# A four-layer language-model tower on one core: the last MoE stage's units, gate and results run on in the head slots, and the tokens are cut in five parts

## The reference

```python
h = take(L0_tok_weight, x)                              # 16384 tokens x 128
h = h + linear_attention(layernorm(h))                  # 8 heads of 16, relu(q), relu(k), clipped denominator
h = h + expert_choice_ffn(layernorm(h))                 # 32 experts, each takes its best 512 tokens
h = h + causal_attention(layernorm(h), Wq, Wk, Wv, Wo)  # 64 sequences of 256, 8 heads of 128
logits = layernorm(h) @ gate_w + gate_b                 # last stage: 8 experts
vals, idx = top_k(logits, 2); w = softmax(vals)
out = h + sum over the 2 picked e of w_e * (relu(x @ w1[e] + b1[e]) @ w2[e] + b2[e])
```

## Time and profile before

| | us |
|---|---|
| median of 3 runs | 2666.74 |
| the profiled execution, its own time | 2664.6 |
| its span, first to last instruction | 2662.9 |
| causal attention with 3 parts of units, first head product to last head sum | 908.4 to 2496.5 |
| gate, scatters and table of the last part | 2496.5 to 2525.8 |
| its 56 units, to the landing of the last output | 2525.8 to 2636.3 |
| six results and the last stores | 2636.3 to 2662.9 |

### The profile page before, as it was taken

One profiled execution on the slowest core, in us unless ns is written; L12 is line 12 of the kernel. 1 busy time (PEld: TensorE's weight loads), 2 busy tenths in 40 slices (PEclk: granted clock), 3 DMA queues, 4 the chain that ended last, 5 costly groups with the idle time before them and its releaser, 6 DMA issues.

```text
span 2662.9 us, 58077 instructions
## 1 busy us (share of the span) xinstructions
PE 2256.9 (85%) x16551; PEld 2003.8 (75%) x16551; DVE 1941.9 (73%) x8859; ACT 1681.3 (63%) x5240; POOL 1178.9 (44%) x1217
## 2 busy tenths in 40 slices
PE   4888878576667599999999999999999999999473
PEld 4777755455555488888888899999989899889463
DVE  4888856644444388888888988788798888888522
ACT  4776745222222377777777788888878788778253
POOL 7555300588888302222222234444436554454343
PEclk9999989777777799999999999999999999999787
DMA  2332310244444520000000155555537754773387
GB/s 79 95 84 80 88 39 1 50 73 78 75 72 74 102 54 26 26 27 29 25 25 25 32 135 151 155 150 152 151 96 223 221 157 112 213 205 105 110 259 216
DMA packets 282605, 271.30 MB, mean 102 GB/s; under 512 B 32795, under 2 KB 232057, under 8 KB 282288
## 3 DMA queue, kind: packets, MB, share of 16 engines
q1 hardware_dynamic: 231600, 195.90, 27.1%
q0 software_dynamic: 46080, 61.16, 10.2%
q10 hardware_dynamic: 4608, 10.52, 1.3%
HBM read 182.69 MB, written 86.84 MB: 101 GB/s over the span
## 4 chain that ended last, share of the span: by engine, by line
PE 48%; DVE 25%; POOL 12%; issue 8%; DMA 3%; SPq 2%; ACT 1%; DVEq 0%; POOLq 0%; ACTq 0%
POOL hbuf L816 7%; PE bank L2148 6%; PE bank L2061 6%; PE bank L2134 5%; PE bank L2069 5%; PE bank L2101 4%; PE bank L2109 3%; POOL xe L808 3%; PE bank L2060 3%; PE bank L2081 3%; PE bank L2083 3%; PE bank L2082 3%; DVE pr_place L1550 2%; DVE nmax L1532 2%; DVE pr_place L1543 2%
## 5 line engine op out<-in xcount | busy, mean ns | idle before, releaser
L856 POOL DMA_INDIRECT spread_rows<-kb,pos x256 | 249.2, 973 | 455.1 <-ACT pr_place L1069 318.1
L870 POOL DMA_INDIRECT zbuf<-pc,kb x232 | 232.4, 1002 | 265.3 <-DVE pc L1712 214.7
L1067 ACT ACTIVATE pr_place<-bank,nmax 128x128 f32<-128x128 f32 x512 | 188.5, 368 | 218.1 <-DVE nmax L1532 215.6
L2061 PE MATMUL bank<-xT,gT 128*128 128x256 f32 x1024 | 306.3, 381 | 0.0
L2069 PE MATMUL bank<-ident,pr_place 128*128 128x128 f32 x1536 | 254.6, 275 | 52.8 <-DVE pr_place L1550 52.4
L2069 PEld LDWEIGHTS bank<-ident,pr_place 128*128 128x128 f32 x1536 | 189.3, 141 | 139.7 <-DVE pr_place L1543 72.0
L1550 DVE COPY pr_place<-bank 128x384 f32<-128x384 f32 x512 | 281.4, 550 | 1.5 <-PE bank L2069 1.4
L2148 PE MATMUL bank<-wvo_part,x_part 128*128 128x512 f32 x768 | 268.3, 457 | 0.0
L1077 ACT ACTIVATE bank<-causal 128x384 f32<-128x384 f32 x512 | 253.4, 495 | 19.7 <-PE bank L2186 3.6
L1531 DVE TENSOR_REDUCE nmax<-bank 128x1 f32<-128x128 f32 x512 | 143.5, 280 | 158.6 <-PE bank L2061 156.8
L2134 PE MATMUL bank<-x_part,wqk_part 128*128 128x256 f32 x1536 | 245.5, 296 | 1.7 <-DVE x_part L1657 1.2
(11 more groups left out here) (322 smaller groups left out, 6276.8 us busy)
## 6 DMA issues: line engine op xcount, KB each, us to landing
pa<-bundle SPq DMA_DIRECT2D x186, 321.0 KB
wu_more<-bundle SPq DMA_DIRECT2D x62, 321.0 KB
junk<-zbuf SPq DMA_DIRECT2D x32, 512.0 KB
kb<-spread_rows SPq DMA_DIRECT2D x232, 65.0 KB
xrow<-xr SPq DMA_DIRECT2D x32, 320.0 KB, 2.5
hbuf<-h SPq DMA_DIRECT2D x32, 256.0 KB, 3.0
hx<-hbuf SPq DMA_DIRECT2D x64, 128.0 KB, 2.8
h3buf<-h SPq DMA_DIRECT2D x64, 128.0 KB
```

The lines of the kernel that those rows point to most:

```text
L2061: pe.matmul(s2[:, P:3 * P], g[:, P:2 * P], xT3[:, p], start=False, stop=True, skip_group_check=True)\
```

## The change

`PORTS` has five parts in place of four: 14, 8, 5, 3 and 2 groups, with 120, 72, 48, 32 and 24 units, 296 in all in place of 288. The list of slots goes on from 512 to 591 (`NI` pairs of 16). `place_steps` gives every step a slot: part 0 from 256, part 1 from 384, part 2 from 464 to 513, part 3 from 514 to 548, part 4 from 549 to 575. The tails written by hand are gone; each engine runs the slot loop to its end, and what belongs to heads is left out after slot 511 or its lag. So the gate of group 31 is in slots 517 to 527, its scatters one a slot in 528 to 535, the last table in 528 to 534 and the last padding in slot 536.

`LOADS` names the slot of each load: four before the unit's own, and for units from 256 on five to seven before it. The rows and weights of units from `RING` = 248 on lie in the buffers of the tail before. Results of groups 0 to 21 stay with POOL in slots below 512. Those of 22 to 26 are loaded by SP in slots 520, 524, 528, 532 and 536, those of 27 to 29 in 555, 559 and 563, and each is added by DVE two slots later. Only groups 30 and 31 come behind the loop. The core of the diff:

```diff
-PORTS = ((0, 13), (13, 21), (21, 26), (26, 32))
+PORTS = ((0, 14), (14, 22), (22, 27), (27, 30), (30, 32))
+NKA = 3
...
+RING = END0 + WR
...
+    steps, at, ends, slot = [], {}, [], 0
     for k, (g0, g1) in enumerate(PORTS):
-        lags = LAGS[k == NK - 1]
+        lags = LAGS[k >= NKA]
+        slot = max(slot, (g1 + 2) * 2 * H1)
         for r in range(NUNS[k] + lags[2]):
...
+            at[slot + r] = len(steps)
+            steps.append([UNIT0[k] + r - d if 0 <= r - d < NUNS[k] else None for d in lags])
+        slot += NUNS[k] + lags[2]
+        ends.append(slot)
...
+        for t, u in SLOT_OF.items():
+            early = u - 4 if t < RING + WR else max(u - 4 - min(3, (t - RING - WR + 2) // 2), (PORTS[portion_of(t)][1] + 1) * 2 * H1 + H1 + 1)
+            LOADS.setdefault(early, []).append(t)
...
+        for k, (g0, g1) in enumerate(PORTS[:-1]):
             for g in range(g0, g1):
+                RESULT_AT[STEP_END[k] + 6 + 4 * (g - g0)] = g
...
             def load_end(t):
+                if q == 0:
+                    sp.wait_ge(head_mm, U)
+                if q >= ER:
                     sp.wait_ge(z_out[(t - ER) % YR], given(t - ER + 1, (t - ER) % YR))
...
+                if q % 2 == 0:
+                    if q < WR:
+                        sp.wait_ge(yu_ready, t - WR + 1)
...
-            for u in range(NB * H1):
+            for u in range(NI * 2 * H1):
...
                 for k in range(NK):
-                    if (i, p, h) == (PORTS[k][1] + 1, 1, 4):
+                    if (i, p, h) == (PORTS[k][1] + 1, 1, 4 if k < NK - 1 else 0):
                         pad_regions(k)
...
+                for t in LOADS.get(u, ()):
+                    (load_unit if t < RING else load_end)(t)
                 if u in RESULT_AT:
                     turn_result(RESULT_AT[u])
-            store_h(NB - 1)
-            late = len(RESULT_AT)
-            turn_result(late)
-            pad_regions(NK - 1)
-            sp.wait_ge(yu_ready, END0)
-            sp.wait_ge(head_mm, NB * H1)
-            for t in range(UNIT0[NK - 1], UNIT0[NK]):
-                load_end(t)
...
+                if i == NG + 1 and p == 0:
+                    scatter(NG - 1, h // TG, h % TG)
                 if u - 2 in STEP_AT and STEPS[STEP_AT[u - 2]][2] is not None:
                     give_unit(STEPS[STEP_AT[u - 2]][2])
...
-                if u - 2 in RESULT_AT:
+                if u - 2 in RESULT_AT and u < U:
                     add_rows(RESULT_AT[u - 2])
...
                         if u - 1 in STEP_AT:
                             unit_out(STEP_AT[u - 1])
                         for k in range(NK):
                             if i == PORTS[k][1] + 1 and p == 0 and h < TABLE_PARTS:
                                 table(k, h)
+                        if u - 2 in RESULT_AT and u >= U:
+                            results(RESULT_AT[u - 2])
```

More of the change, by code:

```diff
@@ L53, in place_steps @@
 def place_steps():
-    steps, at = [], {}
+    steps, at, ends, slot = [], {}, [], 0
     for k, (g0, g1) in enumerate(PORTS):
-        lags = LAGS[k == NK - 1]
+        lags = LAGS[k >= NKA]
+        slot = max(slot, (g1 + 2) * 2 * H1)
         for r in range(NUNS[k] + lags[2]):
[L59 to L64, removed]
+            at[slot + r] = len(steps)
+            steps.append([UNIT0[k] + r - d if 0 <= r - d < NUNS[k] else None for d in lags])
+        slot += NUNS[k] + lags[2]
+        ends.append(slot)
+    return steps, at, ends
 def first(i):
@@ L448, in end_there @@
             q = j % ER
-            return 32 * (j // ER + 1 + (len(range(q, END0, WR)) if q < WR else 0))
+            return 32 * (j // ER + 1 + (len(range(q, RING, WR)) if q < WR else 0))
         xy_mm = sem("xy_mm")
@@ L495, in lm_tower @@
         RESULT_AT = {}
[L496 to L497 removed]
+        for k, (g0, g1) in enumerate(PORTS[:-1]):
             for g in range(g0, g1):
[L499 to L500 removed]
+                RESULT_AT[STEP_END[k] + 6 + 4 * (g - g0)] = g
+        assert list(RESULT_AT.values()) == list(range(PORTS[-1][0]))
         def rounds(eng, one):
@@ L1110, in unit_step, with load_weights, heads @@
                     ins.then_inc(hTu_ready, 1)
-            def heads(i, last):
+            def load_weights(t):
+                q = t - RING
+                k = portion_of(t)
+                j = t - UNIT0[k]
+                act.wait_ge(yu_ready, t - (WR if q < WR else ER) + 1)
+                e = act.value_load(unit_x[j:j + 1, k:k + 1], min_val=0, max_val=E1 - 1)
+                act.dma_start(wu_at(t), bundle[bass.ds(e, 1)].rearrange("a p c -> (a p) c")).then_inc(end_in[q % ER], 16)
+            def heads(i):
                 for p in range(2):
@@ L1127, in heads @@
                                 .then_inc(vo_ready, 1)
-                        if h == 5 and not (last and p == 1):
+                        if h == 5 and n + 1 < NB:
                             turned(n + 1, 1 - p)
@@ L1131, in heads @@
                             exps(u - S_LAG, (h - S_LAG) % H1)
-                        if (p, h) == (1, 5) and there(i - 1):
+                        if (p, h) == (1, 5) and gated(i - 1):
                             gaps(i - 1)
[L1134 to L1161, removed]
+            for i in range(NI):
+                heads(i)
         @block.vector
@@ L1714, in unit_out, with results, slots @@
                     .then_inc(yu_ready, 1)
-            def slots(i, last):
+            def results(c):
+                p = c % 2
+                dve.wait_ge(z_in[p], 32 * (c // 2 + 1))
+                if c >= 2:
+                    dve.wait_ge(out_done[p], 16 * (c // 2))
+                dve.tensor_tensor(res[:, p], zx[:, p, :, 0:C], zx[:, p, :, C:2 * C], ALU.add).then_inc(res_step, 1)
+                dve.wait_ge(res_step, c + 1)
+                dve.tensor_tensor(res[:, p], res[:, p], h3x[:, p], ALU.add).then_inc(res_ready, 1)
+            def slots(i):
                 for p in range(2):
@@ L1720, in slots @@
                         u = H1 * n + h
-                        if h in (1, 2, 3) and not (last and p == 1):
+                        if h in (1, 2, 3) and n + 1 < NB:
                             root = [prep_root, 5 * (h - 1), 1, 1]
-                        elif p == 0 and h in (6, 7) and there(i - 1):
+                        elif p == 0 and h in (6, 7) and gated(i - 1):
                             root = [gate_root, 7 * (h - 6), 1, 2]
@@ L1760, in slots @@
                             finish(n - 1, 1 - p, i, p)
-                        if (p, h) in GATE_SLOTS and there(i - 1):
+                        if (p, h) in GATE_SLOTS and gated(i - 1):
                             GATE_SLOTS[p, h](i - 1)
```

192 lines of the change are left out of this document (66 added, 126 removed).

## The result

The changed kernel takes 2690.76 us (median of 4 runs, 2687.1 to 2692.67) where the kernel before took 2666.73 beside it (4 runs): a ratio of 1.0090, 95% interval 1.0073 to 1.0108. It is slower by 24.0 us. The profiled execution took 2692.07 us, its span is 2689.1, 26.2 above the 2662.9 of before. The forecast was 2681.3: 14.6 us slower.

What follows compares the result with a forecast made beforehand. Behind the heads, DVE's result requests and SP's row loads were taken to wait for each other in a loop. Head phase, results, outputs and end summed to 2677.5, +14.6 on the span: forecast 2681.3 us, range 2642 to 2700.

Steps and rivals of the forecast that it cites:

- the head phase: Up to the last head sum: 11 more unit steps at 0.90 us, 9.9 us, so the sum comes at 2506.4.
- the first result: Behind the heads: SP's store, seven load issues of 7.7 us, then 8.5 us for result 22, at 2523.4.
- The loop: Behind the heads: DVE's result request and SP's row load wait for each other, 14.5 us a turn of four slots.
- Result 23: Behind result 22: its SP slot waits for unit 246's output; 11.4 us, to 2534.8.
- Result 24: Behind result 23: one loop turn and the first scatter of group 31, 1.3 us; at 2550.6.
- Result 26: Behind result 24: unit 256's output, six POOL instructions, padding, landings and load; 34.8 us, to 2585.4.
- Result 27: Behind result 26: output to landing 4.9, 19 issues 20.9, then the result; 34.3 us, to 2619.7.
- Padding: In SP's slots before result 26: 8.35 us for the padding, and 2 us taken for its landing.
- Edits taken at nothing: Gate and table in passing slots, and result adds on DVE beside POOL's scatters (at most 4 us): no cost.
- A: Rival behind the heads: loop hidden, landings covered by loaded units, SP's issue the limit; span 2638.6, time 2642.4; chance 0.17.
- B: Rival behind the heads: loop there, but landings short as in the empty end; 2663.5, no difference; chance 0.18.
- C: Rival behind the heads: long landings, each result among loads SP has just issued; 2705.4; chance 0.08.

Runs made afterwards that it cites:

- e1_again: The kernel after, unchanged, run again beside the other experiments: 2689.88 us, ratio 1.0084.
- e9_four: Against the kernel after: slots run on with the early request, but tokens in the four parts of the kernel before, 288 units: 2668.99 us, ratio 1.0011.
- e3_behind: Against the kernel after: results 22 to 29 taken out of the slots, all ten last results behind the last unit: 2664.67 us, ratio 0.9997.
- e2_late6: Against the kernel after: DVE asks for each late result six slots behind SP's load, not two: 2662.56 us, ratio 0.9987.
- e5_late3: Against the kernel after: DVE asks for late results three slots behind SP's load, not two: 2678.16 us, ratio 1.0039.
- e8_all: Against the kernel after: requests six slots behind, last paddings one by one and awaited in slot 537, row ring of 18 places: 2663.94 us, ratio 0.9989.
- e10_wait: Against the kernel after: requests six slots behind, last paddings one by one, awaited in slot 542; third chip: ratio 0.9998.
- e13_wait: Same kernel as e10_wait, run again on the third chip: ratio 0.9980.
- e11_late4: Against the kernel after: DVE asks for late results four slots behind SP's load, not two; third chip: ratio 1.0033.
- e12_late4: Same kernel as e11_late4, run again on the third chip: ratio 1.0029.

## Why the prediction was right, point by point

The direction and the mechanism held: the time of 2690.8 lies within 2642 to 2700, 9.5 above the forecast. By spans the forecast was 14.6 and 26.2 was measured; three steps carry the 11.6: 7.4 from the head phase and 5.0 from the first result, less 0.8 on the whole way behind it. That the sum came so close is in part luck, as the first point shows. By place, 16.6 of the 26.2 lie before slot 512's transposes, and only 9.6 behind them.

- **The loop.** Predicted 14.5 for a turn; measured 13.9 to result 25, 15.3 to result 28, 13.3 to result 29 (e1_again 14.1, 15.1, 12.8). Its terms were off in ways that nearly cancel: the output's landing 2.90 and 2.96 for 3.7, the result's 7.71 and 5.54 for 6.0. Result 23: 13.0 for 11.4. Result 24: 16.2 for 15.8. Result 26, with the padding: 33.4 for 34.8. Result 27: 33.9 for 34.3. Last landing 16.1 for 16.2, the end 12.3 for 12.6. From result 22 to the end of the span it was 153.3 us, forecast 154.1.
- **The head phase** failed by 7.4: DVE's `finish` of the last head came at 2513.82, not 2506.4. Of this 4.8 were there before slot 240 (see the last section). The stretch of slots 240 to 512 grew by 11.8 against the earlier trace rows where six steps at 0.90 gave 5.4: more steps, but also more results beside steps (22 where 19 stood). The eight profiles of five parts on the first chips, whose slots are the same there, have 947.0 to 951.8, so this execution is near the upper end, and some of the miss is its own. In e9_four, which has the steps and results of before there, it was 938.7, so the growth belongs to the new parts; what each of steps and results costs was not parted. The drained slots gave 3.8 back: 5.9 us against 5.2, where I added 4.5, so the four steps that stand ahead of the last head sum were nearly free there (I had counted five; the fifth is behind it).
- **The first result** failed by 5.0: 22.0 us from `finish` to result 22's adds, forecast 17.0. I had SP stand at slot 517's store, ready. The timeline of SP in the kernel after shows it behind its own issues:

```profile
2515.34 0.34 SPq L646 DMA_DIRECT2D pa<-bundle  x1
2516.54 0.34 SPq L644 DMA_DIRECT2D kb<-spread_rows  x1
2517.63 0.34 SPq L646 DMA_DIRECT2D wu_more<-bundle  x1
2518.01 0.43 SPq L679 DMA_DIRECT2D h3buf<-h  x1
```

  In this stretch a slot has two issues, 2.25 us, while the slots themselves passed in 1.47. SP came to the store 3.8 us after I had it there; seven further issues took 8.2 for 7.7, and the result 9.15 for 8.5. So part of the price of the four drained slots stands in SP's queue, where I had put nothing.
- **Padding** cost near what the earlier trace rows said: 8.01 us of issues for 8.35, and a landing of 1.58 (I took 2). The kernel after, SP's queue and chain:

```profile
2580.74 8.01 SPq L630 DMA_DIRECT2D spread_rows<-padrow  x8
```

```profile
2588.42 1.58 DMA spread_rows<-padrow
```

- **Edits taken at nothing.** The gate and table in slots did not show on the path. The adds on DVE beside POOL's scatters did not either: the scatters behind results 27 and 28 took 0.97 us each, not the 1.35 and 1.50 of the earlier trace rows. The rule of the Trainium skill on that (SBUF — State Buffer, Who interferes with whom) did not come into play, for POOL stood waiting for DVE during the adds. In e3_behind, where one scatter did run beside them, it took 1.32 us.
- **The rivals.** A (hidden, 2642.4) did not come, and e2_late6 shows that it does not come even with the request out of the way. Its span is 19.3 above A's 2638.6: SP had issued the loads of 247 to 250 at 2522.2, not 2514.9, which is 7.3; from there to the end of the last row load it took 109.2 us, where A's sum of SP's issues has 98.3, which is 10.9 more. In this stretch the DMA engines were at 0.92, 0.96, 0.72 and 0.93, a limit that A left out; that it makes all of the 10.9 was not tried. My line that no row showed a landing under 4.6 held for results alone: an output's was 2.11. B and C priced all landings at one end; those read in the chain between results 24 and 29 were 4.6 to 7.7 for results and 2.9 to 4.2 for outputs, so neither end held. The Trainium skill (DMA: Bandwidth & Descriptors, Anatomy of one DMA — SWDGE (gpsimd) path) has about 2 us fixed for a DMA of this kind; 2.90 in a turn of the loop lies nearer to it than my 3.7, the 7.25 of e5_late3 far from it. In the turn of 2.90 no result was on the way, in e5_late3 one was.

## What to carry to other kernels

Before work is moved in among other work, list for the engine that asks in order what stands behind its request, and for the engine that loads in order which output it waits for; if each is behind the other, price one turn of the loop and not the engine's busy time. Placing the request later cost nothing here: six slots in place of two gave back the whole loss without one instruction more or less. Once the loop is gone, ask for the next bound at once (here a DMA share of 0.96). And count what the change costs ahead of the place that it improves: without the loop the part behind slot 512 was 16.9 us shorter than before, but slot 512 began 11.9 us later, and nothing tried came further than 0.2% under the kernel before.

## What the hardware showed that I had not expected

**A start that is 2 us later, and a clock that sometimes falls.** In all five-part kernels POOL's first gather (a DMA that picks rows by index) began at 14.5 to 14.8 us, in both four-part ones at 12.7. The timeline of POOL, kernel before and kernel after:

```profile
12.69 1.17 POOL L762 DMA_INDIRECT vo_place<-in_L_tok_weight_dram,idst  x1 [0.95 <-POOL idst L758]
```

```profile
14.76 1.17 POOL L768 DMA_INDIRECT vo_place<-in_L_tok_weight_dram,idst  x1 [2.66 <-issue]
```

Its constants take 0.36 us longer with a fifth part; the rest is idle time whose cause the trace does not name. From 15 to 60 us the granted clock was 1.00 in the four-part kernels, and 0.93 to 0.96 in seven of the eight five-part profiles of the first chips. The stretch 15 to 60 us of the kernel after and of e8_all:

```profile
15.00:60.00 45.00, 21.99 (x110) 17.96 (x111) 21.70 (x126) 15.94 (x40) 33.13 (x40) 0.96 0.20 53
```

```profile
15.00:60.00 45.00, 23.08 (x118) 18.57 (x119) 21.98 (x126) 17.21 (x42) 33.13 (x40) 1.00 0.20 53
```

These seven kernels reached slot 5 at 927.4 to 928.5 us; e8_all, with the late gather and the full clock, at 923.6, where the kernel before has 923.5 and e9_four 924.8. So some 4 us of the 24 were lost before slot 5 in the kernel after. The clock can be only a part of them. In the kernel after it was 0.50, the level of 1.2 GHz, from 55 to 57 us, after TensorE had worked 0.06 and 0.71 us in the two stretches of 2 us before; in e8_all, with 0.84 and 0.88 us there, it stayed at 1.00. POOL's 33rd gather, behind this stretch, began at 72.3 us in the kernel before, 74.3 in e8_all and 76.2 in the kernel after: 2 us for the late start, 2 more where the clock fell. Where e8_all won back its 2 us was not traced. Nor does the late start always bring the fall: on the third chip one kernel had 1.00 in e10_wait and 0.92 in e13_wait, another 0.92 in e11_late4 and 1.00 in e12_late4, and the two with the full clock reached slot 5 no sooner (977.3 and 982.6 us, against 976.4 and 973.3). The cause stays open.

**Landings follow what is on the way.** The same scatter to `zbuf` landed in 2.90 us in a turn of the loop, in 3.80 among unit loads of the same kernel, and in 7.25 beside a result in e5_late3. The DMA engines carried 303 GB/s over 30 us at a share of 0.96 in e2_late6, where the fullest stretch read of the kernel before had 246 at 0.82.
